# A hybrid block on one core: attention's prologue and mask order changed, the shared expert's two matrices packed into one

## The reference

```
x = x + attention(norm(x))     16 heads of 64, causal, softmax(q k^T / 8) k, then W_out
x = x + ffn(norm(x))           mixture of experts
x = x + state_space(norm(x))   gated, convolution of 3 taps, linear scan
x = x + ffn(norm(x))           the same weights again
ffn(y) = y + shared(y) + the two best of 16 experts, weighted
expert(y) = (silu(y @ wg) * (y @ wu)) @ wd      wg, wu: 128 x 64, wd: 64 x 128
```

## Time and profile before

| | us |
|---|---|
| median of three runs | 757.01 |
| lowest, highest | 753.51, 758.75 |
| the profiled execution | 756.69 |
| its span, first to last instruction | 754.9 |
| PE busy in it | 718.1 |

### The profile page before, as it was taken

One profiled execution on the slowest core, in us unless ns is written; L12 is line 12 of the kernel. 1 busy time (PEld: TensorE's weight loads), 2 busy tenths in 40 slices (PEclk: granted clock), 3 DMA queues, 4 the chain that ended last, 5 costly groups with the idle time before them and its releaser, 6 DMA issues. The chain is left out here.

```text
span 754.9 us, 15021 instructions
## 1 busy us (share of the span) xinstructions
PE 718.1 (95%) x5707; PEld 506.3 (67%) x5707; DVE 450.7 (60%) x1215; ACT 371.2 (49%) x476; POOL 416.8 (55%) x312
## 2 busy tenths in 40 slices
PE   5889999999999999999999897989899999899998
PEld 4666665665666566565656554978788865678887
DVE  6756656766765676676567500545855556766442
ACT  4345555555555555565555351354564343555421
POOL 6256785686578659657755863034644422254543
PEclk9689999999999999999999999999999999999999
DMA  2000010101001001100100111623223000043332
GB/s 70 8 11 20 23 29 19 27 22 27 25 15 29 24 17 25 36 17 15 30 17 18 26 43 57 150 89 100 87 80 105 1 0 1 11 134 100 104 92 74
DMA packets 41276, 33.49 MB, mean 44 GB/s; under 512 B 14002, under 2 KB 32756, under 8 KB 41204
## 3 DMA queue, kind: packets, MB, share of 16 engines
q1 hardware_dynamic: 41204, 32.52, 15.3%
HBM read 23.32 MB, written 1.31 MB: 33 GB/s over the span
## 5 line engine op out<-in xcount | busy, mean ns | idle before, releaser
L392 POOL TENSOR_TENSOR all_x<-all_x,at_probs 128x1024 f32<-128x1024 f32 (+3 forms) x128 | 208.1, 1626 | 18.7 <-POOL all_x L392 0.4
L476 ACT ACTIVATE at_probs<-at_ring 128x1024 f32<-128x1024 f32 x144 | 144.4, 1025 | 108.4 <-PE at_ring L688 108.4
L530 DVE CUSTOM_DVE_ANT_0 at_ring<-at_ring,at_after_query 128x128 f32<-128x128 f32 (+3 forms) x256 | 119.6, 519 | 55.0 <-PE at_ring L642 50.3
L707 PE MATMUL at_out<-at_probs,at_k_nat 128*64 128x512 f32 (+3 forms) x768 | 141.5, 498 | 1.1 <-DVE a_attn_t L556 0.9
L1180 POOL TENSOR_TENSOR m_prod<-m_gate,m_wb 128x512 f32<-128x512 f32 x64 | 83.0, 1305 | 95.8 <-ACT m_gate L1035 86.4
L392 POOL TENSOR_TENSOR all_x<-at_probs 128x768 f32<-128x768 f32 (+1 forms) x32 | 67.3, 2102 | 111.7 <-ACT at_probs L476 111.5
L526 DVE TENSOR_REDUCE at_half_max<-at_ring 128x2 f32<-128x1024 f32 x64 | 78.2, 1225 | 65.0 <-PE at_ring L642 65.0
L707 PEld LDWEIGHTS at_out<-at_probs,at_k_nat 128*64 128x64 f32 x768 | 49.7, 137 | 71.7 <-issue 59.3
L1089 DVE TENSOR_TENSOR m_hid<-m_prod,m_u 128x512 f32<-128x512 f32 x64 | 43.3, 684 | 66.5 <-POOL m_prod L1180 66.3
L955 PEld LDWEIGHTS m_acc<-rest_wd,m_hid 128*128 128x128 f32 x576 | 74.7, 191 | 6.0
L642 PE MATMUL at_ring<-at_kh,at_qh 64*128 64x512 f32 (+3 forms) x384 | 73.1, 406 | 5.6 <-DVE at_ql L517 2.5
(11 more groups left out here) (247 smaller groups left out, 1232.8 us busy)
## 6 DMA issues: line engine op xcount, KB each, us to landing
m_wb<-m_wt_far SPq DMA_DIRECT2D x128, 128.0 KB, 2.9
at_inv<-at_inv_q SPq DMA_DIRECT2D x240, 32.0 KB, 1.8
all_x<-in_L_attn_a_x SPq DMA_DIRECT2D x8, 256.0 KB, 4.1
at_w_raw<-in_L_attn_a_W_qk SPq DMA_DIRECT2D x8, 128.0 KB, 2.6
out<-all_x SPq DMA_DIRECT2D x4, 256.0 KB, 2.4
a_room<-in_L_attn_a_W_out SPq DMA_DIRECT2D x1, 512.0 KB, 4.1
m_raw_wg<-in_L_ffn_experts_wg SPq DMA_DIRECT2D x1, 512.0 KB, 4.2
m_raw_wu<-in_L_ffn_experts_wu SPq DMA_DIRECT2D x1, 512.0 KB, 4.1
```

The costliest lines, as they stand in the source:

```text
L392: return pool.tensor_tensor(sums[:, :, a * P:b * P], left, right, ALU.add)
L476: act.activation(probs[:, :, slot * BANK:(slot + 1) * BANK], pair("S", unit, slot)[:, :, :], ACT.Exp, scale=BETA).then_inc(exp_done, 1)
L530: last = dve.tensor_tensor_reduce(out=sums_ps, in0=sums_ps, in1=after_query[:, BANK - w:BANK], scale=1.0, scalar=MASKED, op0=ALU.add, op1= ...
L707: last = pe.matmul(out_ps[rows(l), o:o + (b - a) * P], k_nat[g % 3][:, j, rows(l)], probs[:, l, at:at + (b - a) * P], start=(j == 0), stop ...
```

## The change

1. Mixtures: the shared expert's gate and up matrices stand side by side in one 128-column block of `wg`; `wu` has 16 slots only. The last step has one set of three matmuls instead of two. ACT's Silu reads the lower 64 rows of the result and writes the upper 64 of `gate`; DVE multiplies by the upper 64 rows of the same bank; `down` uses rows 64 to 127 only. PE waits for that product before it writes that gate bank again. The zero columns and rows and their memsets go.
2. Attention, all units but the first: mask 0 stands before maxima tile 0 and not after it, mask 2 directly behind mask 1, mask 8 directly behind mask 7. Maxima fills 1, 2, 3 are in another order.
3. Attention, first unit: scores and maxima alternate (`FIRST_ROUNDS`), masks right ahead of their scores.
4. Prologue: ACT makes `kh`, then the queries, and the plain copy of the keys last; DVE's two low parts are not separated by statistics; groups 2 and 3 are turned ahead of tile 5; unit 1's keys are projected ahead of tile 7 behind 3 warm-ups, its queries ahead of tile 9; its keys are turned before round 0; 5 warm-ups stand behind `turn_max` in place of the nine behind the last tiles.

```diff
-MAX_FILLS = [[(0, 0, 1, 0), (1, 0, 2, P)], [(3, 0, 4, 0)], [(2, 0, 3, 0)], [(4, 0, 4, 0)], [(5, 0, 4, 0)],
+MAX_FILLS = [[(0, 0, 1, 0), (1, 0, 2, P)], [(4, 0, 4, 0)], [(3, 0, 4, 0)], [(2, 0, 3, 0)], [(5, 0, 4, 0)],
...
-ROUNDS = [[("M", 0), ("S", 0), ("M", 1)], [("mask", 1), ("M", 2), ("S", 1), ("S", 2), ("M", 3)],
+ROUNDS = [[("mask", 0), ("M", 0), ("S", 0), ("M", 1)],
+          [("mask", 1), ("mask", 2), ("M", 2), ("S", 1), ("S", 2), ("M", 3)],
           [("M", 4), ("S", 3), ("S", 4), ("M", 5)], [("M", 6), ("S", 5), ("S", 6), ("M", 7)],
-          [("mask", 7), ("M", 8), ("S", 7), ("S", 8), ("M", 9)]]
+          [("mask", 7), ("mask", 8), ("M", 8), ("S", 7), ("S", 8), ("M", 9)]]
+FIRST_ROUNDS = [[("S", 0), ("M", 0)], [("S", 1), ("M", 1), ("S", 2), ("M", 2)], [("S", 3), ("M", 3), ("S", 4), ("M", 4)],
+                [("S", 5), ("M", 5), ("S", 6), ("M", 6)], [("S", 7), ("M", 7), ("S", 8), ("M", 8), ("M", 9)]]
...
+def rounds(unit):
+    return enumerate(ROUNDS if unit else FIRST_ROUNDS)
 def ring_uses():
-    uses = [("K", 0, 0), ("Q", 0, 0)] + [("M", 0, m) for m in range(3)] + [("T", 0, 0)] + \
-        [("M", 0, m) for m in range(3, NMAX)] + [("K", 1, 0), ("Q", 1, 0)]
+    uses = [("K", 0, 0), ("Q", 0, 0)] + maxima(0, 3) + [("T", 0, 0)] + maxima(3, 7) + [("K", 1, 0)] + maxima(7, 9) + \
+        [("Q", 1, 0)] + maxima(9, NMAX) + [("T", 1, 0)]
...
             if before == "K":
                 pe.wait_ge(hi_done, 2 * u + 1)
+                pe.wait_ge(kt_done, u + 1)
...
                 for n in range(EARLY):
                     norm.high_part(act, n)
+                keys_high(0)
                 norm.root(act, EARLY)
-                keys_high(0)
+                queries_high(0)
                 norm.root(act, EARLY + 1)
-                queries_high(0)
+                keys_to_turn(0)
                 act.preload_act_table_set("natural_log_exp_and_others")
                 natural_keys(0)
                 for n in range(EARLY, GROUPS):
                     norm.high_part(act, n)
+                keys_to_turn(1)
                 keys_high(1)
                 queries_high(1)
+                natural_keys(1)
...
-                norm.low_part(dve, 0)
-                norm.statistics(dve, EARLY)
-                norm.low_part(dve, 1)
-                norm.invert(dve, EARLY)
-                norm.statistics(dve, EARLY + 1)
-                norm.invert(dve, EARLY + 1)
+                for n in range(EARLY):
+                    norm.low_part(dve, n)
+                for n in range(EARLY, GROUPS):
+                    norm.statistics(dve, n)
+                for n in range(EARLY, GROUPS):
+                    norm.invert(dve, n)
...
                 join_maxima(0)
+                queries_low(1)
...
                             if unit == 0:
                                 max_rows(0)
-                                queries_low(1)
...
-                    if m == NMAX // 2 - 1:
+                    if m == 5:
                         for n in range(EARLY, GROUPS):
                             norm.turn(pe, n)
+                    if m == 7:
+                        pair_free(pe, "K", 1)
+                        warm(3, pair("K", 1)[:, 0, :])
+                        project(1, "K")
+                    if m == 9:
+                        project(1, "Q")
                     max_scores(0, m)
-                    if m == NMAX - 3:
-                        pe.wait_ge(norm.low, GROUPS)
-                    if m >= NMAX - 3:
-                        warm(3)
-                project(1, "K")
-                project(1, "Q")
+                turn_keys(1)
+                turn_max(0)
+                warm(5, out_ps)
...
-                                if n in DIAGONAL and ("mask", n) not in row:
+                                if n in DIAGONAL and not unit:
                                     mask(unit, n)
...
+        lower, shared = slice(0, INTER), slice(INTER, P)
...
+                    h = shared if st == LAST else slice(0, P)
                     for t in range(PER):
-                        last = pe.matmul(acc[:, t * P:(t + 1) * P], hid[g % BUFS][:, t * P:(t + 1) * P],
-                                         f.wd[:, st, :], start=(st == 0 and t == 0), stop=(st == LAST),
+                        last = pe.matmul(acc[:, t * P:(t + 1) * P], hid[g % BUFS][h, t * P:(t + 1) * P],
+                                         f.wd[h, st, :], start=(st == 0 and t == 0), stop=(st == LAST),
...
+                    if g >= RING and (g - RING) % STEPS == LAST:
+                        pe.wait_ge(hid_ready, g - RING + 1)
                     up(g_ps[r], f.wg_hi, f.wg_lo, st, n).then_inc(g_ready, 1)
-                    wait(pe, hid_ready, g - RING + 1)
-                    up(u_ps[r], f.wu_hi, f.wu_lo, st, n).then_inc(u_ready, 1)
+                    if st < LAST:
+                        wait(pe, hid_ready, g - RING + 1)
+                        up(u_ps[r], f.wu_hi, f.wu_lo, st, n).then_inc(u_ready, 1)
...
-                    act.activation(gate[g % BUFS][:, :], g_ps[g % RING][:, :], ACT.Silu).then_inc(gated, 1)
+                    out, of = (slice(0, P), slice(0, P)) if g % STEPS < LAST else (shared, lower)
+                    act.activation(gate[g % BUFS][out, :], g_ps[g % RING][of, :], ACT.Silu).then_inc(gated, 1)
...
                     else:
                         dve.wait_ge(gated, g + 1)
-                    dve.wait_ge(u_ready, g + 1)
+                        left, right, h = gate[r], g_ps[g % RING], shared
...
-                    dve.tensor_tensor(hid[r][:, :], left[:, :], u_ps[g % RING][:, :], ALU.mult).then_inc(hid_ready, 1)
+                    dve.tensor_tensor(hid[r][h, :], left[h, :], right[h, :], ALU.mult).then_inc(hid_ready, 1)
```

More of the change, by code:

```diff
@@ L196, with maxima @@
 SUMMED_AT = [1, 2, 5, 4, 4, 6, 7, 8, 10]
+def rounds(unit):
+    return enumerate(ROUNDS if unit else FIRST_ROUNDS)
 def ring_uses():
-    uses = [("K", 0, 0), ("Q", 0, 0)] + [("M", 0, m) for m in range(3)] + [("T", 0, 0)] + \
-        [("M", 0, m) for m in range(3, NMAX)] + [("K", 1, 0), ("Q", 1, 0)]
+    def maxima(a, b):
+        return [("M", 0, m) for m in range(a, b)]
+    uses = [("K", 0, 0), ("Q", 0, 0)] + maxima(0, 3) + [("T", 0, 0)] + maxima(3, 7) + [("K", 1, 0)] + maxima(7, 9) + \
+        [("Q", 1, 0)] + maxima(9, NMAX) + [("T", 1, 0)]
     for unit in range(UNITS):
         more = unit + 1 < UNITS
-        for r, row in enumerate(ROUNDS):
-            if r == 0 and more:
+        for r, row in rounds(unit):
+            if r == 0 and unit and more:
                 uses.append(("T", unit + 1, 0))
@@ L300, in keys_low @@
             eng.wait_ge(hi_done, 2 * unit + 1)
+            eng.wait_ge(kt_done, unit + 1)
             eng.tensor_tensor(kl[unit % 2][:, :], k_t, kh[unit % 2][:, :].bitcast(FP32), ALU.subtract).then_inc(k_low, 1)
@@ L433, in _, with keys, keys_to_turn @@
             def _(act):
-                def keys_high(unit):
+                def keys(unit):
+                    return pair("K", unit)[:, :, :].rearrange("p h c -> p (h c)")
+                def keys_to_turn(unit):
                     act.wait_ge(proj_ready, 2 * unit + 1)
@@ L439, in keys_high @@
                         act.wait_ge(k_low, unit)
-                    bank = pair("K", unit)[:, :, :].rearrange("p h c -> p (h c)")
-                    act.activation(k_t, bank, ACT.Copy).then_inc(kt_done, 1)
-                    act.activation(kh[unit % 2][:, :], bank, ACT.Copy).then_inc(hi_done, 1)
+                    act.activation(k_t, keys(unit), ACT.Copy).then_inc(kt_done, 1)
+                def keys_high(unit):
+                    act.wait_ge(proj_ready, 2 * unit + 1)
+                    act.activation(kh[unit % 2][:, :], keys(unit), ACT.Copy).then_inc(hi_done, 1)
                 def queries_high(unit):
@@ L507, in _ @@
                         if r == NBURST - 1 and unit + 2 < UNITS:
+                            keys_to_turn(unit + 2)
                             keys_high(unit + 2)
@@ L727, in denominators, with warm @@
                                       start=True, stop=True).then_inc(den_ready, 1)
-                def warm(n):
+                def warm(n, bank):
                     for _ in range(n):
-                        pe.matmul(misc[:, 0:P], k.ident[:, :], k.ident[:, :], start=True, stop=True)
+                        pe.matmul(bank[:, 0:P], k.ident[:, :], k.ident[:, :], start=True, stop=True)
                 pe.wait_ge(k.ident_made, 3)
-                warm(WARM_FIRST)
+                warm(WARM_FIRST, misc)
                 norm.turn(pe, 0)
-                warm(2)
+                warm(2, misc)
                 norm.turn(pe, 1)
@@ L758, in _ @@
                     more = unit + 1 < UNITS
-                    for r, row in enumerate(ROUNDS):
-                        if r == 0 and unit < UNITS:
+                    for r, row in rounds(unit):
+                        if r == 0 and 0 < unit < UNITS:
                             turn_max(unit)
```

(1 more changed line is left out.)

18 lines of the change are left out of this document (6 added, 12 removed).

## The result

The changed kernel takes 746.0 us (median of four runs, 744.8 to 747.84); the kernel before, on the same chip, 756.26 (753.51 to 758.75). With this fourth run the median of before is lower than the 757.01 of the first three, from whose profile the forecast subtracts. The ratio is 0.987, 95% interval 0.982 to 0.991: faster by 1.3% (0.9% to 1.8%), and at the forecast of 746.0. No single execution took 746.0: two took 744.8 and 744.85, at a mean granted clock of 0.993, two 747.16 and 747.84, at 0.990 and 0.988. The median is the middle between the pairs. The profiled execution took 747.84 us at a span of 746.0 and is the longest of the four.

What follows compares the result with a forecast made beforehand. The prediction took TensorE, busy 95% of the span and below full clock early, as the bound. Packing -4.6, masks -2.3, prologue and first unit -3.8 sum to -10.7: 756.7 to 746.0 us, 8-in-10 range 741.5 to 751.0.

Steps and rivals of the forecast that it cites:

- Packing: Mixtures: 8 up halves of 0.70 us go (5.6), less 1.0 for 64-row groups: -4.6 us, bounds -2.7 and -5.6.
- The term for the change of shape: Mixtures' 64-row down groups: 0.18 us per change, taken as 0.125 a time, x 8 = 1.0 us.
- The stall for a late product: Mixtures: where DVE is late, PE's stall moves from the up half to the down group, keeping its length.
- Masks: Attention: masks 2 and 8 save 0.18 us a unit, 2.5 over fourteen; POOL's later sums cost 0.2: -2.3 us.
- the reason given: Mask 0's move is worth 0: maxima tile 1 waits anyway for ACT to copy the natural keys.
- what a group of them costs beside that is the first score matmul behind it: Attention: the first score matmul behind masks takes 0.21 us against 0.12, so each joined mask saves 0.09.
- Prologue and first unit: First scores at 36.2 instead of 38.02, unit 1 at 56.4 instead of 60.16: -3.8 us, bounds -6.5 and +8.9.
- 18.7 + 1.5 for a low clock: First unit's length: 18.7 us with scores and maxima alternating, plus 1.5 for part of it at low clock.
- Its waits for POOL and ACT: First unit: waits for the last maxima and the first denominator behind POOL's sums, 1.5 us, between 0 and 3.
- Rival 1: First 60 us give nothing, since at half clock the chain only changes its order: 749.8 us, chance 0.15.
- Rival 2: Mixtures: 64-row groups cost both ways, 0.36 each, so packing gives 2.7: 747.9 us, or 749.3; chance 0.12.
- Rival 3: Clock stays at 1.2 GHz through the first unit, which takes 29.8 us: slower, 758.7 us, chance 0.05.

Runs made afterwards that it cites:

- run 1: The kernel before with the shared expert's packing alone, attention untouched: 753.4 us, ratio 0.997.
- run 4: The changed kernel with the shared expert's down group on all 128 rows, zeros in the 64 weight rows without weights: 744.2 us.
- run 8: The changed kernel with mask 0 alone back between maxima tile 0 and scores 0, from unit 1 on: 747.0 us.
- run 9: The changed kernel with half of each unit's natural keys (head 1) copied by DVE instead of ACT, from unit 2 on: 743.7 us.
- run 10: The kernel of run 9 with mask 0 back between maxima tile 0 and scores 0: 745.0 us.
- run 7: The changed kernel with mask 2 alone back ahead of its scores: 747.3 us.
- run 6: The changed kernel without the prologue's filling matmuls, `warm(3)` ahead of the second keys and `warm(5)` ahead of the first scores: 749.0 us.
- run 5: The changed kernel with its first unit's scores and maxima in the old order: 748.1 us, ratio 0.9905.
- run 3: The kernel before with the new prologue and first unit alone, plus the new order of maxima fills: 751.8 us, ratio 0.993.
- run 2: The kernel before with masks 0, 2, 8 moved and the new maxima fills alone, in all units: 755.3 us, ratio 0.9998.
- run 11: The changed kernel with matmuls added in three later PE waits, two in the last unit, one at mixture 2's start: 744.4 us.
- run 12: The changed kernel with the edits of run 4, run 9 and run 11 together: 740.4 us, ratio 0.979.

## Why the prediction was right, point by point

- **Packing, forecast -4.6, measured -4.0 (run 1).** The 5.6 us of up matmuls went: with the price of 64 rows taken out (run 4), the stretches from mixture 1 to the end are 5.55 us shorter than before. The term for the change of shape, 1.0, measured 1.5 and is what the forecast has too low. The forecast put the transpose behind three of a mixture's four groups; in the trace it is two. One change is paid in those (0.19), both ways where a gate half follows (0.38), and part of it is hidden in a shorter wait (run 4). The stall for a late product moved from the up half to the down group, as forecast, and kept its length: 1.43 us before, 1.45 after.
- **Masks, forecast -2.5 for 14 units and +0.2 for POOL's sums in the last, measured -1.3 and +0.2.** The place of mask 0 is worth 0 (run 8), for the reason given (runs 9 and 10). Mask 8's 0.09 came (that round is 0.08 shorter), mask 2's did not (0.02, run 7). The step that failed is "what a group of them costs beside that is the first score matmul behind it": the row at 174.80 was compared with pairs of its own width, but the pair that really stood ahead of scores 2 without the mask is 128 columns wide too.
- **Prologue and first unit, forecast -3.8, measured -5.6.** Forecast were first scores at 36.2, between 34.7 for a high and 37.1 for a low clock; they came at 35.08, with the clock full from the second matmul of unit 1's keys on (25.55 above). That is 1.1 of the miss of 1.8; the unit, 0.7 shorter than forecast, is the rest. The unit was forecast at 18.7 + 1.5 for a low clock; it took 19.50 at full clock. Its waits for POOL and ACT, guessed at 1.5, took 1.19 and 0.73, and the 1.5 for the clock was not paid because of the change's own filling matmuls: without them (run 6) the unit takes 20.89. The forecast has no term for `warm(5)`.
- **The alternation** of scores and maxima, which is most of the code in the first unit, was not priced apart in the forecast. Run 5 gives it 0.4 us of the 5.6.
- **Rival 1** (the first 60 us give nothing) falls with run 3. **Rival 2** (packing pays little, 0.36 each time) was right in its price for one group in four, not in its sum: 1.5 us, not 2.9. **Rival 3** (low clock through the first unit) did not come: the clock is 1.00 from 26 to 60 us. The rival's own working is off by a little: 16.7 x 1.8 is 30.1, not 29.8. The Trainium skill's page for it (TensorE: Matmul & The Clock Gate, A second HAM failure mode: psum-queue depth-cycling) describes small idles between groups that make the clock go back and forth; here PE is idle for 2.1 of the 20 us from 40 to 60, in several places, and the clock stayed full.
- **That the total met 746.0** to the tenth is luck. In the traces the parts saved 4.0, 1.1 and 5.6, together the 10.7 of the forecast, but its packing is 0.6 too high, its masks 1.2 too high and its prologue with the first unit 1.8 too low: the errors cancel. A dip of the clock near 650 us, which the execution of before did not have and for which the forecast has no term, took 1.7 back in the profiled execution. And 746.0 lies between two pairs of executions, at 744.8 and at 747.2 to 747.8.

## What to carry to other kernels

Price a change in the order of TensorE's work against what will then stand next to each instruction, its width included, and not against the average of its kind. In this kernel halving the rows of a matmul saved nothing and cost the change of shape; where zeros can fill the other half, as in run 4, try that. A covered edit (mask 0) is worth trying again once its cover is removed.

## What the runs showed of the hardware

- A 64-row group of down matmuls between 128-row matmuls costs 0.19 us for each change of shape, and its half of the rows won nothing (run 4: 2.66 against 2.28 us a step).
- The granted clock dips from 2.4 GHz after some waits of 1 to 2 us of TensorE and not after others of the same length: after 1.87 us without work in run 6, not after 2.00 us in run 2; after 1.75 us in the last unit of before, not after the same 1.75 us of after. A dip late in this kernel cost 1.4 to 1.7 us (the last unit takes 36.04 and 36.38 us with one, 34.67 and 34.69 without; from mixture 1 to mixture 2 it takes 160.36 with one, 158.62 to 158.71 without). With matmuls put in the waits the clock was 1.00 in the last unit of both profiles taken (runs 11 and 12), against one of twelve without.
- Totals of single parts (2.4, 0.2 and 5.1 us) don't show their stretch lengths (4.0, 1.2 and 5.6), and the clock in the first 60 us differs from execution to execution: 0.67 to 0.86 at 20 to 40 us in kernels with the same prologue (before, runs 1 and 2). For parts of 1 to 4 us here, distances between rows at full clock decide what medians of four to ten runs can't; where two kernels have the same prologue, comparing executions at equal mean clock helps too (run 5).
